# Delta-rule attention and FFN block: state kept plain by VectorE and spread by ScalarE, with a new spread of the dense matmuls

## What is computed

```
xn = layernorm(x)
q, k = l2norm(heads(xn @ Wq)), l2norm(heads(xn @ Wk));  q *= 32 ** -0.5
v, beta = heads(silu(xn @ Wv)), sigmoid(xn @ Wb)
per head and token t:  delta = (v_t - S^T k_t) * beta_t
                       S = S + k_t delta^T;   o_t = S^T q_t
attn = (rmsnorm(o) * o_norm_weight) @ Wo
ffn  = ((silu(xn @ fp8(gate) * gs) * (xn @ fp8(up) * us)) @ fp8(down)) * ds
out  = x + attn + ffn
```

## Time and profile before

| what | value |
|---|---|
| median of 3 runs | 2276.19 us (2276.04 to 2282.8) |
| profiled execution | 2288.38 us, span 2286.6 us |
| mean granted TensorE clock | 0.992 |
| PE, DVE, ACT, POOL busy | 93%, 85%, 43%, 12% of the span |

### The profile page before, as it was taken

How to read it: one execution, slowest core, us unless ns; L and a number is a source line. 1 busy time by engine, 2 the same in 40 slices (tenths; PEclk the granted TensorE clock), 3 DMA queues, 4 the chain that set the end, 5 groups by cost and what they waited for, 6 DMA issues and landing times.

```text
span 2286.6 us, 82010 instructions
## 1 busy us (share of the span) xinstructions
PE 2122.0 (93%) x36464; PEld 1089.5 (48%) x36592; DVE 1947.2 (85%) x3591; ACT 987.0 (43%) x2525; POOL 267.4 (12%) x519
## 2 busy tenths in 40 slices
PE   2889999999999999999999999999999999999996
PEld 1445454554545455454544545445444444445453
DVE  8988989889898988888878888887888878898886
ACT  4652534435353443535335353342534425354442
POOL 2101011020101102011010101101011020110200
PEclk9999999999999999999999999999999999999998
DMA  7001111001111100111100111001111001111000
GB/s 262 20 3 21 38 21 39 17 7 39 21 38 21 39 12 12 39 21 38 21 11 30 21 38 21 29 12 21 38 22 39 7 16 38 21 38 22 11 12 20
DMA packets 89951, 68.47 MB, mean 30 GB/s; under 512 B 68480, under 2 KB 68480, under 8 KB 89600
## 3 DMA queue, kind: packets, MB, share of 16 engines
q1 hardware_dynamic: 88880, 63.20, 9.7%
q10 hardware_dynamic: 720, 0.03, 0.0%
HBM read 30.72 MB, written 16.78 MB: 21 GB/s over the span
## 4 chain that ended last, share of the span: by engine, by line
PE 84%; DVE 10%; issue 4%; DMA 1%; ACT 0%; SPq 0%; DVEq 0%
PE D L456 25%; PE D L446 23%; PE D L519 13%; PE T L371 12%; PE D L387 7%; PE T L363 4%; DVE state L1386 1%; DVE f_lo L1218 1%; DVE stats L917 1%; DMA qt<-in_L_attn_Wq_dram 1%; DVE outer_v L1232 1%; DVE outer_p L1382 1%; DVE at L1239 1%; DVE at L920 0%; DVE kq L1254 0%
## 5 line engine op out<-in xcount | busy, mean ns | idle before, releaser
L456 PE MATMUL D<-xt,wgu 128*128 128x512 f16 x3072 | 689.4, 380 | 15.9 <-ACT sg L739 6.7
L446 PE MATMUL D<-xt,w_hi 128*128 128x512 f16 x1664 | 493.5, 383 | 26.0 <-DVE w_lo L1004 24.1
L456 PEld LDWEIGHTS D<-xt,wgu 128*128 128x128 f16 x3072 | 291.0, 98 | 365.0 <-issue 10.6
L519 PE MATMUL D<-wd,f_hi 128*128 128x512 bf16 x752 | 286.1, 380 | 17.8 <-issue 15.4
L446 PE MATMUL D<-xt,w_lo 128*128 128x512 f16 x768 | 294.5, 384 | 0.2 <-issue 0.2
L1232 DVE TENSOR_TENSOR outer_v<-mt,at 128x62 f32<-128x62 f32 (+15 forms) x496 | 260.2, 525 | 13.6
L1239 DVE TENSOR_TENSOR at<-at,outer_v 128x62 f32<-128x62 f32 (+15 forms) x496 | 260.9, 526 | 11.8
L446 PEld LDWEIGHTS D<-xt,w_hi 128*128 128x128 f16 x1664 | 160.1, 99 | 217.7 <-issue 33.9
L794 ACT ACTIVATE qt<-T 64x128 f32<-64x128 f32 (+1 forms) x384 | 104.7, 273 | 355.9 <-DVE outer_p L1382 352.9
L519 PE MATMUL D<-wd,f_lo 128*128 128x512 bf16 x656 | 248.6, 379 | 0.8
L729 ACT ACTIVATE kpv<-kpv,rk 128x32 f32<-128x32 f32 x1024 | 231.1, 308 | 35.1 <-DVE kpv L1096 35.1
(11 more groups left out here) (175 smaller groups left out, 2783.1 us busy)
## 6 DMA issues: line engine op xcount, KB each, us to landing
xs<-_attn_hidden_states_dram SPq DMA_DIRECT2D x32, 512.0 KB, 3.4
out_dram<-xs SPq DMA_DIRECT2D x32, 512.0 KB, 3.0
fuse<-in_L_ffn_gate_w_dram SPq DMA_DIRECT2D x2, 768.0 KB, 9.0
xs<-in_L_ffn_up_w_dram SPq DMA_DIRECT2D x2, 768.0 KB, 9.0
f_hi<-in_L_ffn_down_w_dram SPq DMA_DIRECT2D x2, 768.0 KB, 10.4
f_lo<-in_L_ffn_down_w_dram SPq DMA_DIRECT2D x2, 768.0 KB, 12.0
kpv<-in_L_attn_Wk_dram SPq DMA_DIRECT2D x1, 1024.0 KB, 11.5
qt<-in_L_attn_Wq_dram SPq DMA_DIRECT2D x1, 1024.0 KB, 13.7
```

Source lines behind the costliest of these rows:

```text
L446: last = nc.tensor.matmul(D[bank][:, :], w[:, k, cols], xp[:, k, :], start=n == 0, stop=n == len(products) - 1)
L456: last = nc.tensor.matmul(D[bank][:, :], wgu[:, n // 2, c:c + P], (xt_hi, xt_lo)[n % 2][:, n // 2, :], start=n == 0, stop=n == 2 * KT_ - 1)
L519: last = nc.tensor.matmul(D[bank][:, :], (f_hi, f_lo)[n % 2][:, ic, j * P:(j + 1) * P], wd[:, ic, :], start=n == 0, stop=n == 2 * IC - 1)
```

## The change

The state of the chain is kept twice. DVE adds the outer product to a plain `state_sum` (one add of 128x256), and ACT then writes the two-head blocks from it with two scaled copies; `s_ready` comes from ACT, and the wait of ACT's copy `q_out` is now behind these. The layer norm of the next span is applied by ACT (scale `rstd`, bias `shift`); DVE only forms `shift`, two small instructions a span. The dense work is spread anew: 10 instead of 8 matmuls behind each burst of the uw stage, 5 and 8 instead of 7 and 7 in a step of the chain. `fuse_tile` 10 and 11, `low_part` 9 to 11, `silu_gate` 11, `high_part` 11, the squares and the x parts get other places, and four matmuls of projection 6 go ahead of the second gram burst.

```diff
-HIGH_AT, LOW_AT = {1: (0, 1), 3: (2, 3)}, {2: 0, 3: 1, 4: 2, 5: 3}
-SQUARE_AT = {3: (0, 1), 4: (2, 3)}
+HIGH_AT, LOW_AT = {1: (0,), 2: (1,), 3: (2,), 4: (3,)}, {2: 0, 3: 1, 4: 2, 5: 3}
+SQUARE_AT = {2: (0,), 3: (1,), 5: (2,), 6: (3,)}
-APPLY_LATE = {0: 0, 2: 1}
+SHIFT_AT = {0: 0, 1: 1}
-FILL_UW, FILL_CHAIN = 8, 7
+FILL_UW, FILL_CHAIN = 10, (5, 8)
...
-        outer_p = sb("outer_p", [P, 256])
+        outer_p = outer_v[:, 256:512]
+        state_sum = sb("state_sum", [P, BATCH, MS, DH])
+        shift = sb("shift", [P, TILES])
...
                     project(5)
+                    project(6, end=4)
                     grams_of(1)
-                    project(6)
+                    project(6, first=4)
...
-                        fill(fill_at(c, 0), FILL_CHAIN)
+                        fill(fill_at(c, 0), FILL_CHAIN[0])
...
-                        fill(fill_at(c, 1), FILL_CHAIN)
+                        fill(fill_at(c, 1), FILL_CHAIN[1])
...
                     silu_gate(10)
+                    silu_gate(11)
...
                             high_part(10)
-                        if c == 1:
-                            silu_gate(11)
-                        if c == 2:
                             high_part(11)
+                        for j in () if closing else HIGH_AT.get(c, ()):
+                            act.wait_ge(shift_ready, since(BATCH, j // 2 + 1))
+                            act.wait_ge(tt_ready, since(2, 2))
+                            nc.scalar.activation(xn[:, j], xs[:, 1 - par, j, :], ACT.Identity, bias=shift[:, j:j + 1], scale=rstd[:, j:j + 1]).then_inc(xn_ready, 1)
...
-                        act.wait_ge(ds_read, since(STEPS, c + 1))
+                        act.wait_ge(s_summed, since(STEPS, c + 1))
+                        for e in range(2):
+                            last = nc.scalar.activation(state[:, :, :, e, :], state_sum[:, :, :, :], ACT.Copy, scale=of_pair[:, e:e + 1])
+                        last.then_inc(s_ready, 1)
...
-                        dve.wait_ge(tt_ready, since(2, 2))
-                        for j in (2 * b, 2 * b + 1):
-                            layer_norm_apply(j, 1 - par).then_inc(xn_ready, 1)
+                        nc.vector.scalar_tensor_tensor(shift[:, two], mv[:, two, 0], -1.0, rstd[:, two], ALU.mult, ALU.mult).then_inc(shift_ready, 1)
...
                     read_w(7)
+                    fuse_tile(10)
                     low_part(8)
...
                         if c == 0:
-                            fuse_tile(10)
+                            fuse_tile(11)
                         if c == 1:
-                            low_part(9)
                             low_part(10)
-                        if c == 2:
                             low_part(11)
...
-                        for e in range(2):
-                            half = state[:, :, :, e, :].rearrange("p b m d -> p (b m) d")
-                            ins = nc.vector.scalar_tensor_tensor(half, outer_p[:, 0:256].rearrange("p (n d) -> p n d", d=DH), of_pair[:, e:e + 1], half,
-                                                                 ALU.mult, ALU.add)
-                        ins.then_inc(s_ready, 1)
-                        if c == 1:
-                            fuse_tile(11)
+                        nc.vector.tensor_tensor(state_sum[:, :, :, :], state_sum[:, :, :, :], blocks(outer_p), ALU.add).then_inc(s_summed, 1)
+                        if c == 0:
+                            low_part(9)
```

More of the change, by code:

```diff
@@ L82, in fill_at @@
 def fill_at(c, half):
-    return 4 * FILL_UW + (2 * c + half) * FILL_CHAIN
+    return 4 * FILL_UW + c * sum(FILL_CHAIN) + half * FILL_CHAIN[0]
 def dense_order():
@@ L266, in delta_block_kernel @@
         v_step, p_step = sem("v_step"), sem("p_step")
-        q_out = sem("q_out")
+        q_out, shift_ready, s_summed = sem("q_out"), sem("shift_ready"), sem("s_summed")
         low_half, high_half = slice(0, P // 2), slice(P // 2, P)
@@ L963, in _ @@
             one(nc.vector.memset(w_hi[:, :, 3 * DM:], 0.0))
+            one(nc.vector.memset(state_sum[:, :, :, :], 0.0))
             one(nc.vector.memset(state[:, :, :, :, :], 0.0))
@@ L1282, in aggregate, with shift_of @@
                         nc.vector.tensor_scalar(var_e[:, two], mv[:, two, 1], LN_EPS, None, ALU.add).then_inc(var_ready, 1)
-                    def apply_norm(b):
+                    def shift_of(b):
                         if closing:
                             return
+                        two = slice(2 * b, 2 * b + 2)
                         dve.wait_ge(rstd_ready, since(BATCH, b + 2))
-                        dve.wait_ge(tt_ready, since(2, 2))
-                        for j in (2 * b, 2 * b + 1):
-                            layer_norm_apply(j, 1 - par).then_inc(xn_ready, 1)
+                        nc.vector.scalar_tensor_tensor(shift[:, two], mv[:, two, 0], -1.0, rstd[:, two], ALU.mult, ALU.mult).then_inc(shift_ready, 1)
                     def low_x(j):
@@ L1383, in all_spans @@
                         dve.wait_ge(ds_read, since(STEPS, c + 1))
-                        for e in range(2):
-                            half = state[:, :, :, e, :].rearrange("p b m d -> p (b m) d")
-                            ins = nc.vector.scalar_tensor_tensor(half, outer_p[:, 0:256].rearrange("p (n d) -> p n d", d=DH), of_pair[:, e:e + 1], half,
-                                                                 ALU.mult, ALU.add)
-                        ins.then_inc(s_ready, 1)
-                        if c == 1:
-                            fuse_tile(11)
+                        nc.vector.tensor_tensor(state_sum[:, :, :, :], state_sum[:, :, :, :], blocks(outer_p), ALU.add).then_inc(s_summed, 1)
+                        if c == 0:
+                            low_part(9)
                         if c in LOW_AT:
                             low_x(LOW_AT[c])
-                        if c in APPLY_LATE:
-                            apply_norm(APPLY_LATE[c])
+                        if c in SHIFT_AT:
+                            shift_of(SHIFT_AT[c])
                         if c in Q_SUM_AT:
```

## The result

| | kernel before | changed kernel |
|---|---|---|
| median of 4 runs | 2278.7 us (2276.04 to 2282.8) | 2352.9 us (2349.03 to 2356.85) |
| ratio after/before, 95% interval | | 1.0324 [1.0298, 1.0351] |
| profiled execution | 2288.38 us | 2356.85 us, span 2355.1 us |
| mean granted TensorE clock | 0.992 | 0.977 |

The changed kernel is 3.2% slower: 74.2 us, or 4.6 us in each of the 16 spans. The forecast was 2350. The two profiled executions lie 68.5 us apart, 4.3 a span, and the account by stages further down is made from these two. Medians and means are over spans 2 to 15, where nothing else is said. Intervals between bursts are differences of two starts in the timeline of PE.

What follows compares the result with a forecast made beforehand. PE was taken to bound the kernel, with 3 to 4 us idle a span to win. Chain +4.45, uw stage +0.6, holes -0.3 made 4.75 us times 16 spans, 76 us on 2276.2, rounded down to 2350; range 2308 to 2385.

Steps and rivals of the forecast that it cites:

- step 0, first half: Pairs to quads: fuse_tile(10) delays DVE to 3.58 after T, the last w transpose's end; 3.57 us instead of 2.24.
- step 0, second half: Quads to pairs: fuse_tile(11), waiting for a dense matmul, stands ahead of the quads' transpose; 4.37 us instead of 2.41.
- steps 2, 4, 6: Plain chain steps: 4.81 us instead of 4.65, +0.16 each, +0.5 together.
- holes in the chain: Unexplained PE holes in small-matmul bursts, partly taken up by PE's new waits ahead of bursts: -0.3 us a span.
- uw stage: Ten dense matmuls a burst, bursts every 3.79 instead of 3.36 us, partly offset by fewer holes: +0.6 a span.
- rivals B: Only half of step 0's price, one fuse less late or the spread cheap: 2318 us, chance 0.15.
- C: Faster: tile 10's gate ready in time, ten dense cover the wait and holes: 2252 us, chance 0.08.
- D: No change: gains in uw-stage holes equal a smaller loss in step 0: 2276 us, chance 0.05.
- The state loop: Quads to next pairs, one add and two ACT copies: 2.99 us against PE's 2.62, waiting 0.37 every step but the last.
- The collision with POOL: Steps 3 and 5: POOL's down-product add meets the single state add, +0.45 us at most; both steps 5.25.
- The layer norm: "nothing": Moving it from DVE to ACT changes nothing: DVE isn't waited for there, ACT idles 2 to 4 us.
- Rival A: Step 0's two holes drop the PE clock, about 1.7 us a time, 15 to 25 us: 2370 us, chance 0.12.

Runs made afterwards that it cites:

- e1: Changed kernel with fuse_tile(11) moved behind the state sum of step 0 and high_part(11) behind that step's q copy; 2329.8 us.
- e2: Changed kernel with fuse_tile(10) moved back behind the subtraction of step 0, fuse_tile(11) following it; 2322.4 us.
- e3: Changed kernel with fuse_tile(10) behind the subtraction and fuse_tile(11) behind the state sum of step 0; 2302.7 us.
- e4: Changed kernel with the state written by VectorE again, its own order of fuses kept; 2311.4 us.
- e10: Changed kernel in which POOL adds only the first 32 of 512 columns of each down product; 2331.4 us.
- e7: e5 with second statistics behind the last read of w, aggregates in steps 0 and 2, low parts reordered, x parts a step later; 2255.7 us.
- e5: Changed kernel with both fuses of step 0 moved later (behind subtraction and state sum) and the state written by VectorE; 2265.1 us.
- e8: Kernel before with only the next span's layer norm applied by ACT and the x parts one a step; 2269.9 us.
- e9: e7 with the read of the down product ahead of the x part; 2251.9 us.

## Why the prediction was right, point by point

The forecast was 4.75 us a span and 2350; measured were 4.6 and 2352.9. The terms, medians:

| term | predicted | measured |
|---|---|---|
| step 0, first half | 3.57 | 3.64 |
| step 0, second half | 4.37 | 4.33 |
| step 1 | 5.21 | 5.10 |
| steps 2, 4, 6 | 4.81 | 4.70 |
| step 3 | 5.25 | 5.37 |
| step 5 | 5.25 | 5.37 |
| step 7, first half | 1.82 | 1.81 |
| the chain in all | +4.45 | about +4.2 |
| holes in the chain | -0.3 | -0.34 |
| uw stage | +0.6 | +0.24 (mean, spans 2 to 15), +0.4 (mean, all 16) |

**Step 0** was right in size and cause. DVE was free for the pairs' transpose at T + 3.58, to the hundredth as worked out (the gate came 0.04 later and the work behind it took 0.04 less, so the hundredth is luck and the tenth is not); the fuse of tile 11 stood behind the third dense matmul as predicted. e1, e2 and e3 show each cause by itself and that they add. That is 50 of the 74 us, and rivals B (half the price), C and D fall with it. The last span has no first half to pay for, its pairs to quads are 1.89, so this price of 1.8 falls in 15 spans.

**The state loop** was right in kind, and 0.1 a step too dear. The two copies take 0.91 (predicted 0.90), but the handover from ACT to PE is 0.14 (1003.03 to 1003.17), not 0.25. The 0.25 came from one place, ahead of the pairs of step 0, and that place still measures 0.26 in the changed kernel (994.98 to 995.24); the state's handover is shorter, at my lower bound of 0.15. Why the two differ stays open. Steps 2, 4 and 6 thus cost +0.15 in all instead of +0.5. That ACT's rate is no part of the loss also held: its two copies take 0.91, DVE's two adds 0.88; what is lost is the extra add and the extra handover, 0.52 in step 0 and 0.48 in step 1 by e4. The copies' length agrees with the Trainium skill, ScalarE: Activation LUTs, section "What ACT_TABLE_LOAD costs", which puts an ACTIVATE at 186 ns, 0.833 ns a column and 93 ns for a pointer operand, an estimate of 0.49 for this one; the group in the profile after has 0.500:

```profile
L798 ACT ACTIVATE state<-state_sum,of_pair 128x256 f32<-128x256 f32 x256 | 116.1, 500 | 247.2 <-DVE state_sum L1391 247.2
```

**The collision with POOL** was undersized. I allowed +0.45 at most; the add takes up to 1.09 in this span instead of 0.42. POOL and DVE in step 3, changed kernel, which answers to the earlier trace rows:

```profile
1015.70 1.26 POOL L915 TENSOR_TENSOR xs<-xs,fuse 128x512 f32<-128x512 f32 x1 [16.75 <-DVE fuse L1359]
1016.15 1.09 DVE L1391 TENSOR_TENSOR state_sum<-state_sum,outer_v 128x256 f32<-128x256 f32 x1
...
1018.33 0.69 PE L365 MATMUL T<-kq,state 64*64 64x64 f32 x32 [0.87 <-ACT state L798]
```

The term that was mis-sized is "the single add meets the same, +0.45 at most"; it measured 0.67. In the kernel before the two adds were lengthened together by 0.58, and the first of them took all of it (1.06 of the 1.46); what counts is when POOL ends, not how much DVE has to add. With 0.67 in its place, steps 3 and 5 would have been 5.37 with the handover of 0.14, which is what they measure. e10 takes the collision away and returns 21.5 us.

**The uw stage** was oversized: +0.24 over spans 2 to 15 (mean 16.89 against 16.65), +0.4 over all 16, instead of +0.6. Bursts now come every 3.79 (986.79 and 990.58 in the timeline of PE), as worked out. But the kernel before did not keep its 3.36: its three intervals are 3.50, 3.84 and 4.01 in the mean, those of the changed kernel 3.90, 3.99 and 4.11, so that they grew by 0.65 together and not by 1.3. And the way from the last burst to the pairs of step 0, which I held to be fixed, shrank by 0.41 (5.30 to 4.89): the burst comes later, and DVE's work between the reads sets the start of the pairs. e7 moves one pair of statistics out from between them, and there this way is 3.96 in the mean, where e5 has 4.81. The holes for which the profile names no releaser shrank in this stage from 15.8 us over 24 places to 9.1 over 7, 0.4 a span where I had counted on 0.7. In pairs and quads of the chain they went from 6.1 over 16 places to 0.7 over 3: the -0.3 of the prediction was right. Of the 34.3 us that I divided over uw stage and chain, 16.7 lie in the bursts of the projections, outside both; there they are 13.0 now. Why such holes arise was not tried and stays open.

**The layer norm: "nothing"** was wrong by itself. e8 shows that taking it off DVE wins 9 us in the kernel before, by way of POOL's collision in step 3. In the changed kernel the collision is there again for another reason. POOL's add of step 3 starts 2.74 behind the pairs in e8 and in the changed kernel, but with five dense matmuls in the first half the quads, and with them DVE's add to the state, come 0.43 earlier: 3.19 behind the pairs (1012.96 to 1016.15) instead of 3.62 in e8 (median). So the gain did not appear; the two errors hid each other.

**Rival A, the clock,** happened and cost little. In mid-program (150 to 2200 us) the granted clock drops to the lower level of 1.2 GHz 11 times for a few us, against 3 times before, and seven of these begin 0.5 to 1.4 us behind the start of the quads of a step 0, that is behind the first of its two holes and ahead of the second. Windows of the changed kernel over two of these (columns as in the earlier trace rows):

```profile
442.50:446.50 4.00, 3.22 (x18) 1.07 (x20) 2.20 (x5) 1.80 (x5) 0.00 (x0) 0.57 0.02 4
...
1139.00:1142.60 3.60, 2.82 (x19) 0.99 (x21) 2.20 (x5) 1.92 (x5) 0.00 (x0) 0.53 0.03 7
```

and the burst behind the first, in its timeline of PE:

```profile
441.69 0.84 PE L373 MATMUL T<-kpv 32*32 32x64 f32 x64 [1.76 <-DVE kpv L1375]
...
446.37 0.69 PE L365 MATMUL T<-kq,state 64*64 64x64 f32 x32 [0.56 <-ACT state L798]
```

Quads to pairs is 4.68 there instead of 4.29. The slower dense matmuls eat PE's own wait (0.56 is left of 1.61), so a drop costs 0.1 to 0.8 in this half (against the median of the spans without one), 2.4 us for all seven, and not the 1.7 each that I priced. I priced the drop as if PE were the bound, in a place where I had just shown that it was not. The experiments also tell which hole brings it: in e1, which keeps the first alone, five drops stand behind a step 0; in e2, which keeps the second alone, and in e3 and e5, none. TensorE: Matmul & The Clock Gate in the Trainium skill, section "A second HAM failure mode: psum-queue depth-cycling", says that repeated short idles make the clock swing; the trace agrees in 7 of 16 spans, and the time hardly notices. The mean granted clock of the profiled execution, 0.977 against 0.992, is mostly its first 150 us, 55 us at the lower level against 10; the first uw stage still begins at 140.6 against 140.0, so this cost next to nothing.

Together, per span: 4.2 for the chain by its medians, -0.1 for the last span, -0.3 for the holes in the chain, +0.4 for the uw stage, some +0.15 for the clock, about 4.35 or 70 us, against 68.5 between the two profiled executions. The medians lie 74.2 apart; the 6 us more are the place of these two executions among their fellows (the one before is 10 above its median, the changed one 4). Some of the agreement with the forecast is luck: the collision was too cheap in the sum, and the handover and the uw stage too dear.

## What to carry to other kernels

On an in-order engine an instruction that waits holds all behind it: before a piece is moved ahead of a link in a serial chain, work out when its input is ready, on that engine's own clock, and compare with when the link's input is. That sum, made from starts in the timeline, was right to 0.1 us here, and two misplaced instructions of 0.75 us cost 3.2 us in each span. Moving work to an idle engine pays only where the handover is shorter than what it saves, and a loop that fits to the hundredth of a microsecond has nothing to give for one.

## What the runs showed of the hardware

An operation of DVE with two inputs in SBUF that meets POOL's 128x512 add is not merely slowed: it ends a fixed 0.28 us after POOL does. Four places:

| kernel | DVE start, end | POOL end | difference |
|---|---|---|---|
| changed kernel, step 3 | 1016.15, 1017.24 | 1016.96 | 0.28 |
| e7, step 7 | 989.43, 990.71 | 990.43 | 0.28 |
| e9, step 7 | 987.98, 988.98 | 988.70 | 0.28 |
| kernel before, step 3, first add | 1123.59, 1124.65 | 1124.38 | 0.27 |

The last row's add is the first of the two in the earlier trace rows, taken singly. The traces of the kernel before, the changed one and e1 to e9 hold 457 meetings of a subtraction or a state add with the end of such an add. In 456 of them DVE began 0.28 to 1.18 us before POOL's end, and ended 0.279 to 0.286 us after it (the 0.27 of the table is rounding), whenever it had begun; in the one that is left it began 0.13 before the end and kept its 0.43. So DVE seems to make hardly any way while POOL's add lasts, and the price is set by when POOL ends: up to 1.45 us for an operation of 0.42. GPSIMD Engine Reference in the Trainium skill, section "1. Specifications", names contention with DVE instructions that read two inputs from SBUF and gives no amount; the trace agrees and has the amount beside it.

Two things around it. DVE's operations that read PSUM are not touched: transposes of 128x256 keep 0.45 and the add `qt<-qt,T`, with one input in PSUM, its 0.42 while POOL adds. And who begins first goes on: in e9 DVE's x part (two inputs in SBUF, 128x512) begins 0.23 ahead of POOL's add 15 times and keeps 0.68, and POOL's add takes 1.58 instead of 1.27 each time. That the two take turns at something that one of them holds wholly is my reading; the starts and ends are what is shown.
